# Flamingo block with a mixture of experts: accumulating scatters, maxima inside the cross score product, split expert rows turned in half precision

## The reference

```python
q = _ln((x @ Wq + bq).reshape(b, s1, H, HD), qn_w, qn_b)
ctx = _attn(qT, k, v)                 # 112 keys
ctx_dca = _attn(qT, k_dca, v_dca)     # 16 keys
ctx = ctx + DCA_WEIGHT * ctx_dca      # then ctx @ Wo + bo, gated, added to x
...
p = jax.nn.softmax(causal scores, axis=-1)
hid = hidden_states + attn_out
x2 = rmsnorm(hid, ln2_w).reshape(-1, h)
probs = jax.nn.softmax(x2 @ gate_w.T, axis=-1)
top_w, top_i = jax.lax.top_k(probs, TOPK)            # TOPK = 4, normalised
act = jax.nn.silu(g) * u                             # g, u = x2 @ w1[e], 176 each
down = jnp.einsum('tei,ehi->teh', act, w2)
routed = jnp.einsum('te,teh->th', wfull, down)       # four experts' rows per token
return hid + (routed + shared).reshape(b, s, h)      # gated, added to x
```

## Time and profile before

| what | value |
|---|---|
| median of three runs | 1035.87 us (1030.8 to 1036.84) |
| the profiled execution | 1033.32 us, its span 1031.5 us |
| PE busy | 909.6 us, 88% of the span |
| DVE busy | 794.4 us, 77% |
| ACT busy | 632.5 us, 61% |
| POOL busy | 530.3 us, 51% |
| DMA | 84.02 MB, 81 GB/s over the span |

### The profile page before, as it was taken

How to read it: one execution, slowest core, us unless ns; L and a number is a source line. 1 busy time by engine, 2 the same in 40 slices (tenths; PEclk the granted TensorE clock), 3 DMA queues, 4 the chain that set the end, 5 groups by cost and what they waited for, 6 DMA issues and landing times. The chain is left out here.

```text
span 1031.5 us, 24251 instructions
## 1 busy us (share of the span) xinstructions
PE 909.6 (88%) x8457; PEld 639.6 (62%) x8457; DVE 794.4 (77%) x1866; ACT 632.5 (61%) x1571; POOL 530.3 (51%) x602
## 2 busy tenths in 40 slices
PE   3577789999999999999999999999997699999950
PEld 1244456777776676767676777767764378787730
DVE  5688877878788988888898776778666677777666
ACT  3577768777877877778777766666641044444420
POOL 5788863546456464776653354203454334444542
PEclk9576679999999999999999999999998799999995
DMA  5322410101000011121001124032234344444274
GB/s 172 90 75 70 155 42 22 30 22 50 17 22 17 22 50 37 47 67 64 18 14 29 56 81 144 21 91 67 82 117 139 114 133 144 141 143 140 80 285 150
DMA packets 47686, 84.02 MB, mean 81 GB/s; under 512 B 6433, under 2 KB 36385, under 8 KB 47521
## 3 DMA queue, kind: packets, MB, share of 16 engines
q1 hardware_dynamic: 39648, 61.50, 19.1%
q0 software_dynamic: 6912, 19.93, 5.3%
q10 hardware_dynamic: 1008, 1.03, 0.3%
HBM read 52.82 MB, written 31.98 MB: 82 GB/s over the span
## 5 line engine op out<-in xcount | busy, mean ns | idle before, releaser
L659 PE MATMUL ps<-whi,ar 128*128 128x256 f16 (+1 forms) x880 | 248.6, 283 | 15.4 <-DVE ar L1763 9.1
L661 PE MATMUL ps<-whi,ar 128*128 128x256 f16 (+1 forms) x880 | 248.2, 282 | 0.0
L660 PE MATMUL ps<-wlo,ar 128*128 128x256 f16 (+1 forms) x880 | 248.2, 282 | 0.0
L1541 POOL TENSOR_TENSOR ar<-ar,sm 128x512 f32<-128x512 f32 x64 | 69.9, 1092 | 159.5 <-DVE sm L1829 159.5
L1592 POOL DMA_INDIRECT y<-ar,idx x80 | 76.8, 960 | 100.3 <-ACT ar L1419 85.0
L1448 POOL TENSOR_TENSOR sm<-sm,mhalf 128x1 f32<-128x1 f32 (+2 forms) x72 | 125.2, 1739 | 6.0
L659 PE MATMUL ps<-ar 128*128 128x128 f16 (+1 forms) x768 | 117.3, 206 | 7.3 <-DVE ar L1713 5.5
L660 PE MATMUL ps<-ar 128*128 128x128 f16 (+1 forms) x768 | 116.9, 206 | 0.0
L661 PE MATMUL ps<-ar 128*128 128x128 f16 (+1 forms) x768 | 116.9, 206 | 0.0
L659 PEld LDWEIGHTS ps<-whi,ar 128*128 128x128 f16 x880 | 86.5, 98 | 41.4 <-DVE ar L1763 9.8
L659 PE MATMUL ps<-ar,whi 128*128 128x512 f16 x292 | 111.2, 381 | 0.1
(11 more groups left out here) (233 smaller groups left out, 2287.0 us busy)
## 6 DMA issues: line engine op xcount, KB each, us to landing
ar<-xg SPq DMA_DIRECT2D x80, 144.0 KB
ar<-in_wall SPq DMA_DIRECT2D x16, 512.0 KB, 3.7
stg<-in_wall SPq DMA_DIRECT2D x32, 188.0 KB, 2.5
ar<-in_wall SPq DMA_DIRECT2D x8, 608.0 KB, 4.2
whi<-y SPq DMA_DIRECT2D x4, 1024.0 KB, 8.0
wlo<-y SPq DMA_DIRECT2D x4, 1024.0 KB, 17.5
xg<-in_pad SPq DMA_DIRECT2D x1, 2304.0 KB
xg<-x1d SPq DMA_DIRECT2D x4, 512.0 KB, 3.9
```

The lines of the kernel that those rows point to most:

```text
L659: mm(o, l_hi, r_hi, start=start, stop=False, skip_group_check=True)
L660: mm(o, l_hi, r_lo, start=False, stop=False, skip_group_check=True)
L661: return mm(o, l_lo, r_hi, start=False, stop=stop, skip_group_check=True)
L1541: TT(pr, pr, eq4.unsqueeze(2).broadcast_to([P, GB, S]), ALU.mult).then_inc(sem("p_n"), 1)
```

## The change

Four things change.

- **Accumulating scatters.** `y4` is gone. There are two tables, `acc0` and `acc1`, with one row of 256 per token (and 128 for padding). SP fills both with zeros from `pad` late in the start stage. `send` scatters the first tile of a pair into `acc0` and the second into `acc1` with an addition in the DMA. A later scatter into a table must find the earlier one landed, so it waits for it (`y_put0`, `y_put1`). The row index no longer holds the choice, so the routing loses two steps, and `select` and `index` are shorter. At the end a token has two rows instead of four: 16 loads of 256 KB, `mix` is one addition, and `add_z` moves from POOL to VectorE.
- **Maxima inside the score product.** Three slots of `catT` hold the hi·hi, hi·lo and lo·hi pairings, and the fourth holds zeros on the query side and, on the key side, ones that mark the two key sets (`marks`, loaded once). VectorE puts the negative maxima of a quarter into `mx`, at the columns that match the fourth slot, one transpose turns them (`mx_at` gives 40 or 104 columns), and ScalarE copies the eight rows into `catT`. The matmul over 512 columns is gone.
- **Split ahead of the transposes.** ScalarE casts the activations to half precision before they are turned (`cut_tile(u)`), VectorE makes the low part from SBUF (`lo_tile(u)`), TensorE turns three blocks per tile in half precision, and ScalarE copies all six to `m_T` (`copy_tile`). The last 48 rows' hi and lo parts share a block (rows 0 to 47 and 64 to 111).
- **Five down products for six.** The weights of the last 48 rows stand twice in `whi`, so one matmul makes hi·hi and lo·hi of them, and a second one with 48 rows makes hi·lo.

```diff
             def x2_maxima(i, q):
                 pe.wait_ge(sem("xa_mn"), i * NQ + q + 1)
-                for h in range(QH):
-                    last = nc.tensor.transpose(bank16(xs_bank(i, q))[0:2, h * P:(h + 1) * P],
-                                               (a_mn2 if other(i, q) else a_mn)[:, h, :], idn)
-                last.then_inc(sem("xa_mTp"), 1)
+                n = mx_at(q) + 2 * QH
+                nc.tensor.transpose(bank16(xs_bank(i, q))[0:n, 0:P], mx[:, q % 2, 0:n], idn).then_inc(sem("xa_mTp"), 1)
             def x2_exp(i, q):
-                mm(bank(xs_bank(i, q)), seg, shift2 if other(i, q) else shift, start=True, stop=False, skip_group_check=True)
...
             def turn_m(u, b):
-                pe.wait_ge(sem("me_v"), u + (CH + 4))
-                pe.wait_ge(sem("me_lo"), u + (CH + 2))
-                o = bank(MB).rearrange("p (c i t) -> p c i t", c=2, i=2)
+                pe.wait_ge(sem("me_lo"), u + (CH + 3))
+                pe.wait_ge(sem("mT_cut"), u)
+                o = bank16(MB)[:, 0:6 * P].rearrange("p (c i t) -> p c i t", c=3, i=2)
                 for i in range(2):
-                    nc.tensor.transpose(o[:, 0, i, :], m_p[b][:, i, 0:P], idn32)
-                    last = nc.tensor.transpose(o[0:EREST, 1, i, :], m_p[b][:, i, P:EI], idn32)
+                    for n in range(3):
+                        last = nc.tensor.transpose(o[:, n, i, :], m_s[b][:, i, n * P:(n + 1) * P], idn)
             def down_tile(u, b, off):
...
-                    for n in range(2):
-                        c = off[i] + (KC * GU + n * D)
-                        last = three(bank(DB[b])[:, i * D:(i + 1) * D], m_hl[b][:, 0, n, tt], m_hl[b][:, 1, n, tt],
-                                     wcol(whi, c, D), wcol(wlo, c, D), n == 0, n == 1)
+                    three(o, m_hi, m_lo, wcol(whi, c, D), wcol(wlo, c, D), True, False)
+                    mm(o, m_rest, wcol(whi, c_rest, D), start=False, stop=False, skip_group_check=True)
+                    last = mm(o, m_rest[0:EREST], wlo[0:EREST, bass.ds(c_rest, D)], start=False, stop=True,
...
             def x2_maxima(i, q):
                 act.wait_ge(*seen("xa_mTp", i * NQ + q + 1))
-                A((shift2 if other(i, q) else shift)[0:2, :], bank16(xs_bank(i, q))[0:2, 0:512], ACT.Copy).then_inc(sem("xa_mT"), 1)
+                r = slice(mx_at(q), mx_at(q) + 2 * QH)
+                A(catT[r, 0, 4 * (q // 2):4 * (q // 2) + 4, :],
+                  bank16(xs_bank(i, q))[r, 0:P].unsqueeze(1).broadcast_to([2 * QH, 4, P]), ACT.Copy).then_inc(sem("xa_mT"), 1)
             def cut_tile(u, b):
+                act.wait_ge(sem("me_v"), u + (CH + 4))
+                act.wait_ge(sem("mt_ps"), max(0, u - 1))
+                A(m_s[b][:, :, 0:EI], m_p[b], ACT.Copy).then_inc(sem("me_hi"), 1)
+
+            def copy_tile(u, b):
                 act.wait_ge(sem("mt_ps"), u + 1)
                 act.wait_ge(sem("d_ps"), u + (CH + 2))
-                A(m_hl[b][:, 0].rearrange("p c t -> p (c t)"), bank(MB), ACT.Copy).then_inc(sem("me_hi"), 1)
+                A(m_T[b].rearrange("p c t -> p (c t)"), bank16(MB)[:, 0:6 * P], ACT.Copy).then_inc(sem("mT_cut"), 1)
...
                 if u < PAIRS:
                     tanh(u, u % 2)
+                    cut_tile(u, u % 2)
                 if 1 <= u <= PAIRS:
-                    cut_tile(u - 1, (u - 1) % 2)
+                    copy_tile(u - 1, (u - 1) % 2)
...
             def send(u, v):
                 pool.wait_ge(sem("d_bank"), u + 3)
                 pool.wait_ge(sem("idx"), u + 1)
                 apart(pool)
-                for i in range(2):
+                for i, a in enumerate((acc0, acc1)):
+                    if u >= 1:
+                        pool.wait_ge(sem(f"y_put{i}"), 16 * u)
                     nc.gpsimd.indirect_dma_start(
-                        out=y4, out_offset=bass.IndirectOffsetOnAxis(ap=idx[:, 2 * v + i:2 * v + i + 1], axis=0),
-                        in_=ybuf[v][:, i, :], in_offset=None).then_inc(sem(f"y_put{v % 2}"), 16)
+                        out=a, out_offset=bass.IndirectOffsetOnAxis(ap=idx[:, 2 * v + i:2 * v + i + 1], axis=0),
+                        in_=ybuf[v][:, i, :], in_offset=None, compute_op=ALU.add).then_inc(sem(f"y_put{i}"), 16)
...
                         sp.dma_start(xg[NE * CAP:SLOTS, :], pad[P:P + SPARE * P, :]).then_inc(sem("padded"), 16)
+                        for a in (acc0, acc1):
+                            sp.dma_start(a[0:TOK + P, :], pad[0:TOK + P, 0:D]).then_inc(sem("padded"), 16)
                         load_small(0)
...
                     sp.wait_ge(sem("tx_free"), u + 1)
-                    sp.wait_ge(sem("sel_free"), u + 1)
+                    sp.wait_ge(sem("idx"), u - 3)
...
             for m in range(NB // 2):
-                sp.dma_start(yb[m].rearrange("p (a c) -> p a c", a=2), y4[2 * m * S * TOPK:(2 * m + 2) * S * TOPK, :].rearrange(
-                    "(a p k) d -> p a (k d)", a=2, k=TOPK)).then_inc(sem(f"yb{yb_sem(m)}"), 16)
+                for i in range(2):
+                    sp.dma_start(yb[m][:, i, :], sums[i][m // 2, m % 2]).then_inc(sem(f"yb{m}"), 16)
...
-                link(g, 9, TT(rt_t, rt_eq, kio.unsqueeze(1).unsqueeze(1).broadcast_to(b64), ALU.mult))
-                link(g, 10, V.tensor_reduce(rt_k, rt_t, AX.X, ALU.add))
...
             def lo_tile(u, b):
                 dve.wait_ge(sem("me_hi"), u + (CH + 1))
-                TT(m_hl[b][:, 1].rearrange("p c t -> p (c t)"), bank(MB),
-                   m_hl[b][:, 0].rearrange("p c t -> p (c t)"), ALU.subtract).then_inc(sem("me_lo"), 1)
+                TT(m_s[b][:, :, 2 * P:3 * P], m_p[b][:, :, 0:P], m_s[b][:, :, 0:P], ALU.subtract)
+                TT(m_s[b][:, :, P + HALF:P + HALF + EREST], m_p[b][:, :, P:EI], m_s[b][:, :, P:EI],
+                   ALU.subtract).then_inc(sem("me_lo"), 1)
...
             def mix(m):
-                dve.wait_ge(sem(f"yb{yb_sem(m)}"), yb_full(m))
-                V.tensor_reduce(ob[m].rearrange("p (a d) -> p a d", a=2),
-                                yb[m].rearrange("p (a k d) -> p a d k", a=2, k=TOPK), AX.X, ALU.add).then_inc(sem("y_sum"), 1)
+                dve.wait_ge(sem(f"yb{m}"), 32)
+                TT(ob[m], yb[m][:, 0, :], yb[m][:, 1, :], ALU.add).then_inc(sem("y_sum"), 1)
+            def add_z(m):
```

189 lines of the change are left out of this document (93 added, 96 removed).

## The result

The changed kernel takes 1019.39 us (median of 4 runs, 1016.61 to 1023.26) against 1035.36 us (4 runs) on the same chip: ratio 0.9859, 95% interval 0.9833 to 0.9884. It is faster, by 16 us where 40.8 were forecast, and lies 1.4 us above the forecast range.

A forecast was written before the change was run, and what follows sets the result against it. TensorE was taken to bound the attention stage and pairs, VectorE's sums the end, and no engine the start. Terms -20 - 5 + 3 - 0.8 - 18 = -40.8 us gave 992.5 profiled, forecast 995 us, range 976 to 1018.

The forecast's parts named there:

- The pairs: Pairs of expert tiles: cycle from 3.99 to 4.07 us, +3 us over 40 pairs, bounds -13 and +3.
- It is hidden up to 4.07: Pairs: an adding scatter's landing, bounded by 2.5 and 5.0 us, taken to fit within the 4.07 us cycle.
- the second rival: Pairs: dependent adding scatters set the pace, 4.6 us per pair, 21 us more, 1016 us; chance 20%.
- The gap around 48 rows: Pairs: two 48-row products on TensorE pay 0.20 us each for entering and leaving a narrow form, 0.40 added.
- ScalarE's loop: Pairs: ScalarE's loop, now containing VectorE's, sums to 3.4 us, under the 4.07 us cycle.
- The attention stage: Cross attention there: 0.47 us saved on TensorE per quarter, 44 quarters 20.7 us, a little back as waits; -20 us.
- the earlier groups are hidden beside TensorE: Routing: two dropped steps save 0.8 us before the last rows' scatter; for earlier groups they save nothing.
- The start: Cross attention in the start: 20 quarters with a shorter chain save between nothing and 13 us; taken as -5 us.
- The end: End: 16 VectorE additions of 0.68 us replace eight reductions of 3.57; -18 us, between -15 and -20.
- No fill was late: Start, rival: zero fills take 26 us instead of 13, ScalarE and TensorE wait some 8 us, 1003 us; chance 4%.
- the attention stage didn't give back most: Attention stage, rival: TensorE idles for VectorE, only a third kept, 13 us less gain, 1008 us; chance 9%.
- The slow case: Pairs, rival: scatters make the kernel over 1% slower, from 5.3 us per pair, 1046 us; chance 7%.

The follow-up runs named there:

- plain_chain: The changed kernel with scatters writing rows in place of adding, each still waiting for the one before in its table (sums left out): 995.47 us.
- plain_full: plain_chain with the fifth down product over all 128 rows in place of 48 (adds a lo x lo term): 982.68 us.
- rt_back: The changed kernel with the two dropped routing steps put back, their result not used: 1024.12 us.
- only_maxima: The kernel before with only the maxima in the cross score product, nothing else of the change: 1019.69 us.
- late_fills: The changed kernel with its two zero fills issued in the attention stage in place of the start: 1019.75 us.
- three_slack: The changed kernel with three tables in place of two, buffers freed as early as in the changed kernel: 1019.56 us.

## Why the prediction was wrong

**The pairs, +27.5 us for +3.** The step that failed is "It is hidden up to 4.07, and I take it as hidden, because reading 1 KB rows back should cost part of a second trip, not a whole one." It was bounded between 2.5 and 5.0 us and took 4.13 in the link shown and 4.2 by the median, with 0.3 of hand-over ahead of the next. The comparison was wrong in a second way: 4.07 us of room was set against the landing alone, without the hand-over, so the room was 3.8. The part's other half, that POOL itself is held 0.60 us longer per scatter, wasn't thought of at all. plain_chain shows that the addition alone makes the difference, 24 us. Three tables, which all but end POOL's waits for its tables, took 12.8 of these back in the pairs; how the rest divides between POOL's longer hold and the buffers that are freed later stays open. This was the second rival, "the scatters set the pace", at 4.6 us per pair and 1016 us, with 20%: the mechanism, its sign in the trace (POOL waits for `acc`, 53 times of 80) and its size are as it stands there, 4.59 and 1019.39 us. The range ended at 1018. The 3 us from its 1016 to 1019.39 are about what the attention stage fell short. With 2.5 us plain and no row that showed an addition, the nearer bound had no more reason than the other.

**The gap around 48 rows, right.** Rows and plain_full agree with 0.21 us on either side, plain_chain with the cycle: 4.08 us in most pairs and +3.7 in all, for a forecast of 4.07 and +3. ScalarE's loop, counted at 3.4 us, was at least not above 3.6: the pairs went down to 3.59 by the mean.

**The attention stage, -15.7 us for -20.** The price per quarter was too high: TensorE's busy time in the stage fell from 581.1 to 564.2 us, 0.39 us for each of 44 quarters, not 0.47. Of these 17 us some 4 came back as waits, where "a little" was forecast. And "the earlier groups are hidden beside TensorE" failed: VectorE's burst isn't hidden, since TensorE waits for the subtraction behind it. The trace before had that wait already, for the mask product, three times, up to 2.2 us:

```profile
PE ps L873 <- issue: 5.3, 3, 2.2
```

By the three places where the kernel before falls back, the two steps account for 2.9 of the 15.7 us and the maxima for the other 12.8. The parts aren't independent, though: the maxima alone gave 8.0, and beside them the steps are worth 5.5 (rt_back) to 7.6 us (only_maxima) in this stage, where the forecast had nothing for the earlier groups and 0.8 us for the last. Two wrong sizes partly cancelled.

**The start, -1.3 us for -5.** The profiled starts of the kernels with the new maxima lie between 146.8 and 151.0 us, against one of 152.1 before, so the gain is 1.1 to 5.3; the changed kernel's profile is at the short end. The three longest starts had the lowest granted clocks (0.59 and 0.60), but 150.2 and 149.8 us came at 0.75 and 0.85, so the clock alone doesn't order them. The forecast is within the spread, and a single trace can't size this term. late_fills rules out that two fills hold back the start.

**The end, -20.5 us for -18.** The additions are 0.68 us each and nearly all back to back, as said; the last scatter landed 3.6 us after its start at 995.60, 1.1 later than the plain one of the earlier trace rows, as was allowed for.

**The other rivals.** No fill was late with two tables, and the attention stage didn't give back most. The slow case needed 5.3 us per pair and wasn't met.

## What to carry to other kernels

A scatter that adds is a chain when each must wait for the last one to its table: its landing and hand-over are a bound on the loop, and they belong into the sum beside each engine's cycle, at the dearer bound when no row shows the addition. A gap that a profile puts down to "issue" isn't yet the engine's own time: set its end against the end of what the instruction needed, and look for a stretch where that came early (0.30 us here, not 0.66). Where an engine that others wait for works off a burst, look for steps of it that can go ahead of a wait of its own: moving two steps of 0.42 us was worth 7 us here, about as much as removing them.

## What the runs showed of the hardware that was not expected

- An indirect scatter of 128 rows of 1 KB holds POOL for 0.96 us and lands 2.5 us after its start (median); with addition it is 1.56 and 4.2 us (3.6 to 5.9), in 96 packets more. Rows of 512 bytes hold POOL just as long.
- Two scatters in a row leave a gap of 0.30 us on POOL, also across two pairs (three_slack, after 972.86). Where a scatter waits for ScalarE's store, it starts 0.80 us after the store's end (33 of 40 pairs there).
- VectorE and POOL additions of 512 fp32 elements with two inputs in SBUF stretch each other from 0.68 to 1.74 us and from 1.26 to 2.17; in these stretches the one that started first kept its length. The Trainium skill, "SBUF — State Buffer", "Who interferes with whom", says that a VectorE instruction with two SBUF inputs contends with a GpSimd instruction that reads SBUF; these rows agree, and the kernel is 5.5 us faster with both kinds on one engine, part of which may be the hand-over.
